# Gradient stages of a test-time-trained layer: the output weight's gradient made as 128 by 512 in three float32r passes

## The reference, cut to what matters

```python
def loss_fn(p):
    h = jax.nn.swish(k_ttt @ p['gate']) * (k_ttt @ p['val'])
    pred = h @ p['proj']
    return jnp.mean((pred - v_ttt) ** 2)
for _ in range(TTT_STEPS):                      # 2
    grads = jax.grad(loss_fn)(theta)
    theta = {kk: _muon_update(theta[kk], grads[kk]) for kk in theta}
```

## Time and profile before

| | us |
|---|---|
| median of 3 executions | 2073.51 (2066.87 to 2074.04) |
| profiled execution, its own time: first to last instruction (span) | 2067.8 |
| TensorE busy in the span | 1793.5 (87%) |
| VectorE busy | 1595.5 (77%) |
| ScalarE busy | 1344.5 (65%) |
| GpSimd busy | 706.0 (34%) |

### The profile page before, as it was taken

The page is one execution under the profiler, slowest core; times in us unless marked ns, Lnnn a source line. Parts: engine busy times, 40 slices in busy tenths (PEclk is TensorE's granted clock), DMA queues, the critical chain, the costliest instruction groups (busy, mean ns, idle before and its releaser), DMA issues. The chain is left out here.

```text
span 2067.8 us, 37433 instructions
## 1 busy us (share of the span) xinstructions
PE 1793.5 (87%) x12604; PEld 1437.4 (70%) x12604; DVE 1595.5 (77%) x4173; ACT 1344.5 (65%) x3106; POOL 706.0 (34%) x666
## 2 busy tenths in 40 slices
PE   8999999999999999997387587999899998942782
PEld 6777777777777777776277345888688877722772
DVE  6999999999999999995675675777577766668324
ACT  6888888888888888885456465666366643521323
POOL 0111121111111111121247603999189951000572
PEclk9999999999999999999699788999999999965886
DMA  7000000000000000003175300000000000040444
GB/s 238 1 2 1 1 2 1 1 2 1 1 2 1 1 2 1 2 1 95 28 126 137 74 7 1 1 1 1 1 1 1 1 1 5 2 140 13 110 87 94
DMA packets 64928, 61.52 MB, mean 30 GB/s; under 512 B 10698, under 2 KB 54708, under 8 KB 64612
## 3 DMA queue, kind: packets, MB, share of 16 engines
q1 hardware_dynamic: 52276, 41.50, 6.8%
q0 software_dynamic: 10384, 16.59, 5.0%
q10 hardware_dynamic: 2080, 1.05, 0.2%
HBM read 40.12 MB, written 18.73 MB: 28 GB/s over the span
## 5 line engine op out<-in xcount | busy, mean ns | idle before, releaser
L188 POOL TENSOR_TENSOR x<-x,scaled 128x512 f32<-128x512 f32 x128 | 167.6, 1309 | 784.8 <-DVE scaled L500 784.8
L486 DVE TENSOR_TENSOR probT<-turn_ps,probT 128x512 fp32r<-128x512 f32 x512 | 335.6, 687 | 58.8 <-ACT probT L384 52.0
L399 ACT ACTIVATE prob<-prob,negmax 128x512 f32<-128x512 f32 x512 | 374.0, 736 | 4.3 <-DVE negmax L480 4.3
L480 DVE CUSTOM_DVE_ANT_0 prob<-score_ps,bias 128x512 f32<-128x512 f32 x512 | 341.0, 684 | 1.7 <-issue 0.9
L384 ACT CAST probT<-turn_ps 128x512 fp32r<-128x512 f32 x512 | 282.4, 595 | 10.6 <-PE turn_ps L273 1.9
L303 PE MATMUL work_ps<-probT,val 128*128 128x512 f32 x1024 | 258.5, 394 | 1.2 <-DVE probT L486 1.1
L259 PE MATMUL score_ps<-k,q 64*128 64x512 f32 x1536 | 228.5, 417 | 2.8 <-DVE negmax L480 2.1
L303 PEld LDWEIGHTS work_ps<-probT,val 128*128 128x128 f32 x1024 | 187.5, 188 | 42.0 <-DVE probT L486 3.0
L259 PEld LDWEIGHTS score_ps<-k,q 64*128 64x128 f32 x1536 | 128.0, 188 | 52.5 <-DVE negmax L480 37.4
L318 PE MATMUL work_ps<-wo,ctxT 128*128 128x128 f32 x1024 | 146.1, 286 | 0.7 <-ACT ctxT L391 0.7
L318 PEld LDWEIGHTS work_ps<-wo,ctxT 128*128 128x128 f32 x1024 | 123.9, 191 | 26.8 <-issue 22.8
(11 more groups left out here) (514 smaller groups left out, 4319.6 us busy)
## 6 DMA issues: line engine op xcount, KB each, us to landing
ew<-L_ffn_fc_weight SPq DMA_DIRECT2D x32, 256.0 KB, 3.4
bias<-bias_line SPq DMA_DIRECT2D x16, 448.0 KB, 8.8
mid_rows<-row SPq DMA_DIRECT2D x40, 128.5 KB, 3.8
last_rows<-row SPq DMA_DIRECT2D x40, 64.0 KB
rows_dram<-qk SPq DMA_DIRECT2D x1, 2304.0 KB, 18.8
x_rows<-x SPq DMA_DIRECT2D x4, 512.0 KB, 6.8
acc_dram<-zero POOLq DMA_DIRECT2D x1, 2048.0 KB, 16.2
out<-x SPq DMA_DIRECT2D x4, 512.0 KB
```

The costliest lines, as they stand in the source:

```text
L188: pool.tensor_tensor(mine, mine, scaled[a][:, :, :], ALU.add).then_inc(added, 1)
L399: act.activation(mine, mine, ACT.Exp, bias=negmax[p % 2][:, i, a:a + 1], scale=-1.0, accum_out=total[p % 4][:, i, a:a + 1]).then_inc(exp_d ...
L480: dve.tensor_tensor_reduce(prob[p % 2][a][:, i, :], score_ps[i % 2][a][:, :], bias[:, h, first:first + SEQ][:, ::-1], -1.0, 3.0e38, ALU.ad ...
L486: dve.tensor_tensor(turned(1, g), as_turned(g), turned(0, g).bitcast(F32), ALU.subtract).then_inc(turned_lo, 1)
```

## The change

The output weight's gradient is made the other way round, as `dp` turned over times `h`, 128 by 512, in three float32r passes like the other two, and one tile later (tile o instead of l). For that `dp` and `h` are split: ScalarE makes the high parts, VectorE the low ones. The high part of the keys moves from GpSimd to ScalarE. GpSimd multiplies the slope by `vc` in place, so that the buffers `w` go. `s` has three buffers instead of four, `h` two, and the parts of `h` three. On VectorE, `du_lo` comes ahead of `dpT_lo`. In `newton_schulz` the gradient of `proj` is now taken as the other two are, straight from PSUM, and its turned pieces by the transposes.

In the diff, cut to its core, the pieces stand in this order: GpSimd's step (`sum_keys` is `ks`, `low_keys` is `ks_lo`, which waits for ScalarE's high part) and the slope's product; TensorE, behind `dh`; ScalarE, behind `dpT_hi` and ahead of `s`, then behind `hT` and ahead of `du_hi`; VectorE, behind `dpT_lo` and ahead of the slope.

```diff
...
-                    keys(n - 2)
+                    sum_keys(n - 2)
                     weigh_slope(n - 1)
+                    low_keys(n - 2)
                     low_dv(n - 2)
...
-                pool.tensor_tensor(w[m % 2][:, :], c1[m % 2][:, :], vc[m % 2][:, :], ALU.mult).then_inc(w_ready, 1)
+                pool.tensor_tensor(c1[m % 2][:, :], c1[m % 2][:, :], vc[m % 2][:, :], ALU.mult).then_inc(w_ready, 1)
...
-                    for c in range(HC):
-                        mm = pe.matmul(dwp_ps[:, c, :], h[l % RING][:, columns(c)], dp[l % 2][:, :], start=l == 0 and c == 0,
-                                       stop=l == TILES - 1, skip_group_check=True)
-                    mm.then_inc(dwp_done, 1)
+                if live(o):
+                    edges = {"start": o == 0, "stop": o == TILES - 1, "across": True}
+                    pe.wait_ge(dp_lo, o + 1)
+                    pe.wait_ge(h_lo, o + 1)
+                    three_passes(dwp_ps[:, :], whole(dp_parts[o % 2]), h_parts[o % H_RING], **edges).then_inc(dwp_done, 1)
...
+                    act.wait_ge(dp_ready, l + 1)
+                    if l >= 2:
+                        act.wait_ge(dwp_done, l - 1)
+                    act.copy(dp_parts[l % 2][0][:, :], dp[l % 2][:, :]).then_inc(dp_hi, 1)
+                if live(m):
+                    act.wait_ge(h_ready, m + 1)
+                    if m >= H_RING:
+                        act.wait_ge(dwp_done, m - H_RING + 1)
+                    act.copy(h_parts[m % H_RING][0][:, :], h[m % 2][:, :]).then_inc(h_hi, 1)
...
+                    act.wait_ge(k_summed, l + 1)
+                    if l >= 2:
+                        act.wait_ge(dwv_done, l - 1)
+                    act.copy(ks_parts[p][0][:, :], ks[p][:, :]).then_inc(k_hi, 1)
...
+                    dve.wait_ge(dp_hi, l + 1)
+                    if l >= 2:
+                        dve.wait_ge(dwp_done, l - 1)
+                    dve.tensor_tensor(dp_parts[p][1][:, :], dp[p][:, :], dp_parts[p][0][:, :].bitcast(F32), ALU.subtract).then_inc(dp_lo, 1)
+                if live(m):
+                    r = m % H_RING
+                    dve.wait_ge(h_hi, m + 1)
+                    if m >= H_RING:
+                        dve.wait_ge(dwp_done, m - H_RING + 1)
+                    dve.tensor_tensor(h_parts[r][1][:, :], h[m % 2][:, :], h_parts[r][0][:, :].bitcast(F32), ALU.subtract).then_inc(h_lo, 1)
```

More of the change, by code:

```diff
@@ L1492, in ttt_grads @@
     dwg_ps, dwv_ps, dwp_ps = grad_ps
-    RING = 4
+    RING, H_RING = 3, 3
     with ExitStack() as st:
@@ L1500, in ttt_grads @@
         th, vc, c1 = (sb(n, [P, HID]) for n in ("th", "vc", "c1"))
-        s, h = ([core.sb(st, f"{n}{i}", [P, HID]) for i in range(RING)] for n in "sh")
-        w = sb("w", [P, HID])
-        hT, dp, dpT = sb("hT", [P, HC, P]), sb("dp", [P, D]), two_parts("dpT", [P, P])
+        s, h = [core.sb(st, f"s{i}", [P, HID]) for i in range(RING)], sb("h", [P, HID])
+        h_parts = [parts(f"h{i}", [P, HID]) for i in range(H_RING)]
+        hT, dp, dp_parts, dpT = sb("hT", [P, HC, P]), sb("dp", [P, D]), two_parts("dp", [P, D]), two_parts("dpT", [P, P])
         du, dv, du_parts, dv_parts = sb("du", [P, HID]), sb("dv", [P, HID]), two_parts("du", [P, HID]), two_parts("dv", [P, HID])
@@ L1508, in ttt_grads @@
                  "h_turned", "hT_ready", "pred_done", "dp_ready", "dp_turned", "dpT_hi", "dpT_ready", "dh_done", "du_ready", "dv_ready",
-                 "du_hi", "dv_hi", "du_lo", "dv_lo", "dwp_done", "dwg_done", "dwv_done", "w_hi", "w_lo")
+                 "du_hi", "dv_hi", "du_lo", "dv_lo", "dp_hi", "dp_lo", "h_hi", "h_lo", "dwp_done", "dwg_done", "dwv_done", "w_hi", "w_lo")
         (k_summed, k_hi, k_lo, u_done, v_done, s_ready, th_ready, v_copied, h_ready, c_ready, slope_ready, w_ready,
          h_turned, hT_ready, pred_done, dp_ready, dp_turned, dpT_hi, dpT_ready, dh_done, du_ready, dv_ready,
-         du_hi, dv_hi, du_lo, dv_lo, dwp_done, dwg_done, dwv_done, w_hi, w_lo) = (core.sem(n) for n in names)
+         du_hi, dv_hi, du_lo, dv_lo, dp_hi, dp_lo, h_hi, h_lo, dwp_done, dwg_done, dwv_done, w_hi, w_lo) = (core.sem(n) for n in names)
         block = st.enter_context(nc.Block())
@@ L1520, in _, with sum_keys @@
         def _(pool):
-            def keys(l):
+            def sum_keys(l):
                 p = l % 2
@@ L1525, in keys, with low_keys @@
                 pool.tensor_tensor(ks[p][:, :], qk[:, l, D:2 * D], keep["shift"][:, D:2 * D], ALU.add).then_inc(k_summed, 1)
-                pool.wait_ge(k_summed, l + 1)
+            def low_keys(l):
+                p = l % 2
+                pool.wait_ge(k_hi, l + 1)
                 if l >= 2:
                     pool.wait_ge(dwv_done, l - 1)
-                pool.tensor_copy(ks_parts[p][0][:, :], ks[p][:, :]).then_inc(k_hi, 1)
-                pool.wait_ge(k_hi, l + 1)
                 pool.tensor_tensor(ks_parts[p][1][:, :], ks[p][:, :], ks_parts[p][0][:, :].bitcast(F32), ALU.subtract).then_inc(k_lo, 1)
@@ L1535, in weigh_slope @@
                 pool.wait_ge(v_copied, m + 1)
-                if m >= 2:
-                    pool.wait_ge(du_ready, m - 1)
-                pool.tensor_tensor(w[m % 2][:, :], c1[m % 2][:, :], vc[m % 2][:, :], ALU.mult).then_inc(w_ready, 1)
+                pool.tensor_tensor(c1[m % 2][:, :], c1[m % 2][:, :], vc[m % 2][:, :], ALU.mult).then_inc(w_ready, 1)
             def low_dv(l):
@@ L1585, in _ @@
                     for c in range(HC):
-                        mm = pe.transpose(hT_ps[:, columns(c)], h[m % RING][:, columns(c)], ident[:, :])
+                        mm = pe.transpose(hT_ps[:, columns(c)], h[m % 2][:, columns(c)], ident[:, :])
                     mm.then_inc(h_turned, 1)
@@ L1660, in _ @@
                 m, l, o = n - 1, n - 2, n - 3
[L1661 to L1665, removed]
                 if live(o):
@@ L1671, in _ @@
                     dve.tensor_tensor(du_parts[p][1][:, :], du[p][:, :], du_parts[p][0][:, :].bitcast(F32), ALU.subtract).then_inc(du_lo, 1)
+                if live(l):
+                    p = l % 2
+                    dve.wait_ge(dpT_hi, l + 1)
+                    if l >= 2:
+                        dve.wait_ge(dh_done, l - 1)
+                    dve.tensor_tensor(dpT[p][1][:, :], pred_ps[:, 1, :], dpT[p][0][:, :].bitcast(F32), ALU.subtract).then_inc(dpT_ready, 1)
+                    dve.wait_ge(dp_hi, l + 1)
+                    if l >= 2:
+                        dve.wait_ge(dwp_done, l - 1)
[6 more added lines that the diff above has]
+                    dve.tensor_tensor(h_parts[r][1][:, :], h[m % 2][:, :], h_parts[r][0][:, :].bitcast(F32), ALU.subtract).then_inc(h_lo, 1)
                 if live(m):
@@ L1676, in _ @@
                     if m >= 2:
-                        dve.wait_ge(w_ready, m - 1)
+                        dve.wait_ge(du_ready, m - 1)
                     dve.scalar_tensor_tensor(c1[p][:, :], s[r][:, :], -1.0, th[p][:, :], ALU.add, ALU.mult).then_inc(c_ready, 1)
@@ L1684, in _ @@
                     dve.wait_ge(w_ready, l + 1)
-                    dve.tensor_tensor(du[p][:, :], dh_ps[:, :], w[p][:, :], ALU.mult).then_inc(du_ready, 1)
+                    dve.tensor_tensor(du[p][:, :], dh_ps[:, :], c1[p][:, :], ALU.mult).then_inc(du_ready, 1)
                     if l >= 2:
@@ L1690, in _ @@
                     dve.wait_ge(pred_done, m + 1)
+                    if m >= 2:
+                        dve.wait_ge(dp_turned, m - 1)
+                        dve.wait_ge(dp_lo, m - 1)
                     dve.tensor_tensor(dp[m % 2][:, :], pred_ps[:, 0, :], v[:, m, :], ALU.subtract).then_inc(dp_ready, 1)
@@ L1694, in _ @@
                     dve.wait_ge(v_copied, n + 1)
-                    if n >= RING:
-                        dve.wait_ge(dwp_done, n - RING + 1)
-                    dve.tensor_tensor(h[n % RING][:, :], s[n % RING][:, :], vc[n % 2][:, :], ALU.mult).then_inc(h_ready, 1)
+                    if n >= 2:
+                        dve.wait_ge(h_turned, n - 1)
+                        dve.wait_ge(h_lo, n - 1)
+                    dve.tensor_tensor(h[n % 2][:, :], s[n % RING][:, :], vc[n % 2][:, :], ALU.mult).then_inc(h_ready, 1)
 def newton_schulz(core, keep, grad_ps):
@@ L1724, in newton_schulz @@
         weights = (projT, gate, val)
-        x_ps = [flat(dwp_ps[:, :, :]), dwg_ps[:, :], dwv_ps[:, :]]
+        x_ps = [dwp_ps[:, :], dwg_ps[:, :], dwv_ps[:, :]]
         s_ps = [x[:, 0:P] for x in x_ps]
@@ L1733, in newton_schulz @@
         block = st.enter_context(nc.Block())
-        first = [flat(XT[0][:, :, :]), X[1][:, :], X[2][:, :]]
-        second = [X[0][:, :], flat(XT[1][:, :, :]), flat(XT[2][:, :, :])]
         nth = lambda i, m: M * i + m + 1
@@ L1745, in _ @@
             for m in (0, 2):
-                act.activation(first[m], x_ps[m], ACT.Copy, scale=scales[m]).then_inc(copied, 1)
+                act.activation(X[m][:, :], x_ps[m], ACT.Copy, scale=scales[m]).then_inc(copied, 1)
```

(11 more changed lines are left out.)

## The result

The changed kernel takes 2108.03 us (median of 4; 2104.46 to 2110.69) against 2071.91 for the kernel before (4 runs). The ratio is 1.0168, with a 95% interval of 1.0139 to 1.0197: slower by 1.7%, 36 us. The profiled execution has a span of 2109.0, 41.2 above that of before. From the start of the first pass of `u` to the start of the last pass of `dwv` the two gradient stages and what lies between them went from 419.1 us (1265.75 to 1684.89) to 455.9 (1271.06 to 1726.92), 36.7 more. The first stage also begins 5.3 us later, behind work that both kernels have in common, and what follows the stages is 0.8 shorter.

What follows compares the result with a forecast made beforehand. TensorE bounds the kernel before, the port shared by VectorE and GpSimd the changed one: 62 intervals at 0.51 us (31.6) plus fills (2.7) add 34 us, giving 2105 us between span and median bases, range 2088 to 2118.

Steps and rivals of the forecast that it cites:

- The ledger of the port: Gradient stages: VectorE's two-SBUF-operand operations and GpSimd's share a port; holds per tile go from 5.34 to 5.86 us.
- TensorE's 0.21 less: `dwp` on TensorE: eight passes of 0.90 us become three of 0.69 in all, 0.21 less per tile.
- The walk through a tile, 6.30: One steady gradient tile, followed with gaps at the port: 6.33 or 6.26 us by order, 6.30 taken, 0.51 above 5.79.
- The walk of the other order: Same steady tile with GpSimd's `ks_lo` taking the port ahead of VectorE's `h`: 6.33 us.
- The fill, 1.35 twice: Start of each gradient stage: `h`, `h_hi` and `h_lo` go before the first `c`, 1.35 us more, 2.7 for both.
- The sum, +34: Whole kernel: 62 steady intervals at 0.51 give 31.6 us, the two fills 2.7, together +34 us.
- the drains: End of the gradient stages, on `dv_lo` and three passes: costed at nothing.
- what lies between the stages: The Newton-Schulz stage, turning the same 128 by 512 in the other direction: costed at nothing.
- its base: Time before the change: span 2067.8 gives 2101.8, median 2073.51 gives 2107.5; the middle, 2105 us, was taken.
- ScalarE's loop: Rival: `dp_hi` and `h_hi` ahead of `s` make ScalarE's loop the bound at 5.74 us, about 2070, no change; chance 0.07.
- TensorE as the bound: Rival: TensorE stays the gradient stages' bound, 0.21 us shorter per tile, 2057 or 2063 us, faster by 0.5%; chance 0.03.
- Holding the port for the whole instruction: Rival: every port operation holds it for its full duration, 7.13 us a tile, +86, 2154 us; chance 0.01.

Runs made afterwards that it cites:

- the six passes: Changed kernel with the three passes of `dwp` made twice: span 2107.7 us, most tiles 6.36 us, some twenty of 62 intervals 6.41 to 6.44.
- the runs on each alone: Two edits of the changed kernel: ScalarE's `h_hi` on 256 of 512 columns, span 2108.0 us; TensorE's three `dwp` passes made twice, span 2107.7 us.
- half of `dv_lo`: Changed kernel with GpSimd's `dv_lo` made on 256 of 512 columns from the third tile on: a tile every 5.81 us, span 2074.2 us.
- `h` from PSUM: Changed kernel with VectorE's `h` reading `v` in PSUM instead of its copy `vc`: a tile every 6.09 us, span 2082.5 us.
- the keys back: Changed kernel with the keys' high part made by GpSimd again instead of ScalarE: a tile every 6.46 us, span 2109.3 us.

## Why the prediction was right

It gave 2105 us in a range of 2088 to 2118, slower at 0.90; 2108.03 was measured. Its steps, one by one:

- *The ledger of the port.* Right. The holds that it read from the kernel before return in the kernel after: 0.55 for `h` (`ks_lo` 1.00 against 0.45), 0.15 for `dp_lo` (`ks`, issued at 1344.48, is late by 0.06, so it begins at 1344.54, and `dp_lo` began in effect at 1343.49 + 0.90 = 1344.39), which was an estimate between 0.15 and 0.33. Laid end to end from `h` at 1341.81, the holds of the prediction give the six late starts of that tile (`ks_lo`, `du_lo`, `dv_lo`, `dp_lo`, `ks`, `h_lo`) within 0.03 us.
- *TensorE's 0.21 less.* Right (0.90 to 0.70), and hidden, as the six passes show.
- *The walk through a tile, 6.30.* The mechanism was right, the size 0.07 short. Of the two orders that it allowed, `h` ahead of `ks_lo` is what happened (1341.81 and 1341.82), for which the walk gave 6.26. The missing 0.11 is one term: it set the second `c` 0.60 behind the first, as for two operations that have nothing to do with each other. The second reads what the first writes and waits for its end: 1345.46 to 1346.17, 0.71. The kernel before already showed it, 1270.02 to 1270.73. The walk of the other order, which the slower tiles of the six passes show, is short by nearly the same, 6.33 against 6.43.
- *The fill, 1.35 twice.* From the first pass of `u` to the first tile's second `c`: 4.98 before, 6.36 after, 1.38 more; in the second stage 4.84 and 6.07, 1.23 more.
- *The sum, +34.* In the stages 36.7: the 62 intervals grew by 34.4 (391.9 against 357.5) where the walk gave 31.6, the two fills by 2.6 where it gave 2.7, the drains shrank by 0.4, and what lies between the stages stayed (34.6 us); both of these were put at nothing. The forecast lies 3 us under the measurement, some 2 of them by the sum and 1.3 by its base, the middle between a span and a median (2070.7, against a median of 2071.91 in the end).
- *The rivals.* ScalarE's loop and TensorE as the bound are out by the runs on each alone. Holding the port for the whole instruction is out: it needed 7.13 us a tile, and 6.37 was measured. The Trainium skill's page "SBUF — State Buffer", section "Who interferes with whom", named the right pair of engines and the right kind of operand. The "whole instruction", which its section "SBUF: two separate sides" states for such operations too, is longer than the 0.55 of 0.68 us that the rows show.

The steps say more than the sum: in the runs in which VectorE has no idle time, a tile takes VectorE's 4.93 us plus what its rows are longer than the operation alone, for the change (1.44, 6.37), half of `dv_lo` (0.27 + 0.34 + 0.27, 5.81), `h` from PSUM (0.90 + 0.27, 6.10 against 6.09 measured), and the keys back (0.27 + 0.90 + 0.27 + 0.09, 6.46). This is bookkeeping, as nothing else can fill a tile there; what tests the theory is which rows grew and shrank with each edit.

## What to carry to other kernels

Before giving VectorE or GpSimd more to do, add up the holds of GpSimd's operations and of VectorE's operations with two SBUF operands, in one tile, and compare the sum with the tile. The sum is a floor: with 5.86 us of holds a tile took 6.37 in one order and 6.10 in another. The busy shares of the two engines don't show it, since a blocked operation counts as busy. An operation whose duration varies with what the other engine does is the sign to look for. Where the sum is too large, take an operand from PSUM if it is there anyway, and put the operations that don't use the port (one operand in PSUM) beside GpSimd's long ones; here neither was enough alone (6.09 and 6.10), and both together were (5.60).

## What the runs showed of the hardware that was not expected

A short operation can pay most: `dp_lo`, 0.28 us by itself, took 1.18 because `dv_lo` had the port, more than the 512-column operations around it lost. And six passes instead of three on an engine with 0.8 us of slack per tile left most tiles as they were (6.37 and 6.36 us). Some twenty of them took 0.07 more, those in which the other of two operations came first at the port.
